# Two remainder tiles of the second experts put into one stationary tile, more last blocks kept on chip, and the mask built later

## The chip, the cores and the metric

One core of one Trainium2 chip runs the kernel. The metric is the device time of the kernel in microseconds (us); lower is better. Three runs of the kernel before gave 1200.51, 1204.14 and 1206.46 us, so the median is 1204.14 us.

## What is computed

Two graph layers on 625 nodes of 256 features with 20,000 edges. Each layer is an attention over edges, a mixing part and a mixture-of-experts part that sends each node to its two best experts. This change touches the two expert parts and the mask that lies between them.

```python
# first experts: 16 experts, hidden size 512; second experts: 8 experts, hidden size int(8/3*256) = 682
hidden = silu(h1) * h2                       # h1 = x @ w1[e], h2 = x @ w2[e]
expert_out = hidden @ w3[e]                  # weighted by the router's two best and summed
...
e = einsum('ehd,ehd->eh', q[src], k[dst]) * scale       # second layer's attention, over edges only
ex = exp(e - segment_max(e, dst)[dst])
...
hh = silu(flat @ w1[e].T) * (flat @ w3[e].T)            # second experts
out = out + weights[:, e:e + 1] * (hh @ w2[e].T)
```

## The kernel before, in words

**Experts as blocks.** The function `experts` exists once for each engine and is called for "e0" (first experts) and "e1" (second experts). The 1250 choices (625 nodes, two each) are laid out in blocks of 128 slots, each block of one expert: 25 blocks in e0 (`NBLK0`), 17 in e1 (`NBLK1`). `block_steps` runs blocks 0 to 3 unrolled, then loops over four at a time, and then the last ones unrolled (from block 20 in e0, from block 12 in e1). So every engine has a `step(b)`, and the engines meet through semaphores alone.

**One step of TensorE.** `row_nodes(b+3)` makes the node numbers of a later block, `turn_rows(b+1)` transposes the gathered rows of the next block (L737), `hidden(b)` makes the two input products (L750), and `output(b-1)` makes the output product of the block before (L761). All products are float32; the trace shows two records for each. In e1 the hidden size 682 gives five tiles of 128 columns and one of 42 (`TILES1`), in two units: tiles 0 to 3, then tiles 4 and 5 (`UNITS1`). `hidden` goes through the unit for q=0 (into banks 1 and 2) and then for q=1 (banks 3 and 4). So in each block's second unit TensorE does: tile 4 and tile 5 of the first matrix, tile 4 and tile 5 of the second, each for two halves k of the 256 inputs.

**One step of VectorE.** In this order: `node_ids(b+3)` (L1528, cast of the node numbers, from which GpSimd gathers that block's rows), `select(b+4)`, the product of silu and the second matrix (L1541), `copy_y(b-1)` (L1572, the output of the block before, out of PSUM), and for the last blocks `spread_rows(b)` (two operations at L1561 and one at L1565, which make a 128x625 matrix of weights that brings the block's slots back to the nodes). The first `spread_rows` waits for `row_info`.

**ScalarE and the row information.** ScalarE copies the turned rows (L1879), makes silu (L1899), and stores the output of a finished block to DRAM (L1884, `slot_y`). `fetch_info` (L1917) loads `row_info`, two rows of 1250 numbers broadcast to 128 partitions, at the start of ScalarE's step 20 in e0 and step 12 in e1.

**The two ways back to the nodes.** Outputs of the early blocks are stored to `slot_y`; when the last of these stores has landed, GpSimd issues ten indirect gathers from it (L2085, in `choices`, after the row gathers of all blocks on the same queue), and VectorE adds them to x in five pairs (L1595). Outputs of the last `KEPT` blocks (4 in e0, 2 in e1) stay on chip: TensorE multiplies each by its weight matrix (`combine`, L783, five products for a block) into PSUM, and VectorE adds these sums (L1599) after the gathered ones. Then come the layer normalization (e0) or the output (e1).

**The weights.** SyncE loads each block's input weights (`exw`, L2190) into one of two slots as soon as `hidden` of the block two before is done, and its output weights (L2181). One float32 row of e1's input weights has 4 x 682 = 2728 numbers.

**The mask.** `cnt` holds the logarithm of edge counts. After its last block in e0, and before `copy_y(24)`, VectorE makes a bfloat16 mask in `mask_words` (five operations, L1586) and turns `cnt` into the additive mask of the second layer's attention (five more, L1589).

**What follows e0.** Layer normalization, `to_fm("xnT2")` on TensorE, `from_fm("xnT2")` on ScalarE and VectorE (L959), then products "gq" and "gk" (L486), whose second halves VectorE takes out of PSUM (L1614, L1618).

Of the kernel before, what the change touches and what calls it, by code (L numbers as in the profile page):

```python
# [20 lines left out]
ALU = mybir.AluOpType  # L21
# [9 lines left out]
N, D, E = 625, 256, 20000  # L31
# [73 lines left out]
FOLDS = 5  # L105
KEPT = {"e0": 4, "e1": 2}
PLAIN = 4
NBLK0 = (2 * N - NE0) // SLOTS + NE0
HT0, HT1 = 128, 128
TILES0 = [(m, min(HT0, HID0 - m * HT0)) for m in range((HID0 + HT0 - 1) // HT0)]  # L110
TILES1 = [(m, min(HT1, HID1 - m * HT1)) for m in range((HID1 + HT1 - 1) // HT1)]
UNITS0 = [TILES0]
UNITS1 = [TILES1[:4], TILES1[4:]]
# [56 lines left out]
def build(nc, x_in, src_in, dst_in, rows_in, vec0_in, vec1_in, fb_in, w0_in, w1_in, w2_in, mixw_in, exp0_in,  # L170
          exp0o_in, exp1_in, exp1o_in, exp1r_in, rope_in, out):
    ctx = ExitStack()
    with ctx:
# [149 lines left out]

        exw = arena[:, 0:2 * 4 * HID1].rearrange("p (s n) -> p s n", s=2)
        at = 2 * 4 * HID1
        exo = arena[:, at:at + 2 * 5 * D].rearrange("p (s n) -> p s n", s=2)
# [30 lines left out]
        def y_of(k, s):  # L357

            return ys[:, s, :] if k < 2 else ys_last[:, k - 2, :]

# [81 lines left out]
        def _(pe):  # L442
# [271 lines left out]

            def experts(name, nblk, units, w_in, w_out, n_out):

# [24 lines left out]
                def hidden(b, s):  # L741
                    pe.wait_ge(sem(f"{name}_in{s}"), (b - s) * 8 + 16)
                    pe.wait_ge(sem(name + "_xsT"), b + 1)
                    for j, tiles in enumerate(units):
                        buf = j if nu == 2 else s
                        after(pe, sem(name + "_mul"), b * nu + (j - 1))
                        for q in range(2):
                            for i, (m, rows) in enumerate(tiles):
                                for k in range(K2):
                                    mm = pe.matmul(banks[1 + 2 * q + buf][0:rows, i * SLOTS:(i + 1) * SLOTS],  # L750
                                                   w_in(s, q, k, m, rows), xsT[:, s, k, :],
                                                   start=(k == 0), stop=(k == 1))
                        mm.then_inc(sem(name + "_hid"), 1)
# [21 lines left out]
                def combine(b, s):  # L775
# [6 lines left out]
                    for t in range(T):  # L782
                        pe.matmul(kept_sum(t), row_hots[:, k, t * P:(t + 1) * P], y_of(k, s), start=(k == 0),  # L783
                                  stop=True, skip_group_check=True).then_inc(sem("combined"), 1)
# [95 lines left out]
            def l2_scores(i, m, h):  # L880

                for c, off, w, _ in chunks_upto(m + 1):
# [15 lines left out]
            experts("e1", NBLK1, UNITS1,  # L898
                    lambda s, q, k, m, rows: exw[:, s, (q * 2 + k) * HID1 + m * HT1:(q * 2 + k) * HID1 + m * HT1 + rows],
                    lambda s, m: exo_r[:, s, :] if m == 5 else exo[0:HT1, s, m * D:(m + 1) * D], 2)  # L900


        @block.vector
        def _(dve):
# [581 lines left out]
            def experts(name, nblk, units, shift_logits, shares, then):  # L1486
# [43 lines left out]
                def step(b, q):  # L1530
# [6 lines left out]
                    for j, tiles in enumerate(units):  # L1537
                        buf = j if nu == 2 else s
                        dve.wait_ge(sem(name + "_silu"), b * nu + (j + 1))
                        for i0, m0, n, rows in runs(tiles):  # L1540
                            ins = v.tensor_tensor(hid[0:rows, s, m0:m0 + n, :],  # L1541
                                                  banks[3 + buf][0:rows, i0 * SLOTS:(i0 + n) * SLOTS]
                                                  .rearrange("p (m n) -> p m n", n=SLOTS),
                                                  silu[0:rows, buf, i0:i0 + n, :], ALU.mult)
# [8 lines left out]
                def spread_rows(b):  # L1553
# [4 lines left out]
                    after(dve, sem("spread"), kept_before(name) + k)  # L1558
                    first, second = (f.rearrange("p (t n) -> p n t", t=T) for f in (row_hots[:, k, :], other_hots))
                    for j, hots in enumerate((first, second)):  # L1560
                        own.note(v.scalar_tensor_tensor(hots, rows_slot[j], slot_cols[:, k:k + 1], rows_weight[j],  # L1561
                                                        ALU.is_equal, ALU.mult))
                    own.fence()
                    first = row_hots[:, k, :]
                    v.tensor_tensor(first, first, other_hots, ALU.add).then_inc(sem("spread"), 1)  # L1565
# [17 lines left out]
                block_steps(dve, nblk, step)  # L1583
                if name == "e0":
                    for m in range(T):
                        own.note(v.tensor_scalar(nmask[:, m, :], cnt[:, m, :], -1.0, -BIG, ALU.is_lt, ALU.mult))  # L1586
                    own.fence()
                    for m in range(T):
                        own.note(v.scalar_tensor_tensor(cnt[:, m, :], cnt[:, m, :], HD ** 0.5, nmask[:, m, :], ALU.mult,  # L1589
                                                        ALU.add))  # L1590
                copy_y(nblk - 1, (nblk - 1) % 2)
# [17 lines left out]
            layernorm(x, xn, 1e-5, (sem("xn"), 3 * T), stats_of=())  # L1609
            from_fm("xnT2", fa)  # L1610
            for c, (off, w, _) in enumerate(CHUNKS):
                bank, freed = got(dve, ("gq", 1, c))
# [128 lines left out]
        def _(act):  # L1741
# [129 lines left out]
            def experts(name, nblk, units):  # L1871
# [15 lines left out]
                def step(b, q):  # L1887
# [6 lines left out]
                    for j, tiles in enumerate(units):  # L1894
                        buf = j if nu == 2 else s
                        act.wait_ge(sem(name + "_hid"), b * nu + (j + 1))
                        after(act, sem(name + "_mul"), b * nu + (j - 1))
                        for i0, m0, n, rows in runs(tiles):
                            ins = a.activation(silu[0:rows, buf, i0:i0 + n, :],  # L1899
                                               banks[1 + buf][0:rows, i0 * SLOTS:(i0 + n) * SLOTS]  # L1900
                                               .rearrange("p (m n) -> p m n", n=SLOTS), ACT.Silu)
# [395 lines left out]
```

## Time and profile before

| | |
|---|---|
| median of three runs | 1204.14 us (1200.51 to 1206.46) |
| the profiled execution's own time | 1199.38 us |
| its span in the trace | 1197.6 us |
| TensorE busy | 958.0 us, 80% |
| VectorE busy | 857.0 us, 72% |
| ScalarE busy | 465.5 us, 39% |
| GpSimd busy | 466.9 us, 39% |
| input weights of e1, each block | 1364 KB, 17 loads |
| input weights of e0, each block | 1024 KB, 25 loads |

Times in the trace count from the start of the span. A row of the timeline has the start, the duration, the engine, the line, the operation, what is written and read, the count of merged records, and in brackets how long the engine was idle before and what ended it. Consecutive matmuls overlap, so the distance from start to start tells what one costs, and not the duration. The first experts run from about 644 to 803 us, the second from about 1022 to 1183 us.

### The profile page before, as it was taken

Reading aid. Unit: us, or ns where it says so; the run is one execution under the profiler, and the core shown is the slowest. Engines: PE = TensorE matmul, PEld = TensorE weight load, DVE = VectorE, ACT = ScalarE, POOL = GpSimd, SP = SyncE. Lnnn points to the kernel's source line nnn. Section 1 sums busy time; section 2 is a strip of 40 time slices with the busy share of each in tenths; the row PEclk is TensorE's granted clock in tenths of the full one; section 3 lists DMA queues with packets and bytes.
Section 4 is the critical chain, followed back from the end, with each engine's and each line's share of the span. In section 5 each row is a group of like instructions: output and inputs, shape, how many; then the busy total and the mean of one; then the engine's idle time right before and its main releaser. Section 6 shows DMA issues by size and latency. Waiting matters only on the chain. (4 is left out here: it accounts for less than half of the span.)

```text
span 1197.6 us, 19285 instructions
## 1 busy us (share of the span) xinstructions
PE 958.0 (80%) x6570; PEld 829.1 (69%) x6570; DVE 857.0 (72%) x1934; ACT 465.5 (39%) x791; POOL 466.9 (39%) x374
## 2 busy tenths in 40 slices
PE   4277999679989889974736999976891894999995
PEld 2256798568878778854735999864691683788884
DVE  5457459869887779887987888584879547655514
ACT  1154565557859577527511111101460260111110
POOL 2437878887787778850002222150000000211104
PEclk9688999889999999997866999997996896899998
DMA  8942232322322222129505999870000002777763
GB/s 284 292 145 69 52 73 55 83 47 60 74 62 58 61 61 69 34 44 245 142 22 192 335 322 323 319 246 22 1 2 0 1 2 71 260 268 264 268 240 93
DMA packets 58236, 157.47 MB, mean 131 GB/s; under 512 B 23830, under 2 KB 33227, under 8 KB 49907
## 3 DMA queue, kind: packets, MB, share of 16 engines
q1 hardware_dynamic: 25500, 116.04, 29.8%
q0 software_dynamic: 25056, 24.10, 9.0%
q10 hardware_dynamic: 7610, 16.46, 4.1%
q8 instruction: 37, 0.61, 0.2%
q14 instruction: 33, 0.26, 0.1%
HBM read 136.12 MB, written 20.12 MB: 130 GB/s over the span
## 5 line engine op out<-in xcount | busy, mean ns | idle before, releaser
L2075 POOL DMA_INDIRECT arena<-row_tab,ids x42 | 57.8, 1376 | 503.2 <-DVE ids L1528 500.6
L2030 POOL DMA_INDIRECT pair_scores<-sc_ring,idx_ring x160 | 213.6, 1335 | 61.9 <-issue 48.0
L750 PE MATMUL bank<-arena 128*128 128x128 f32 (+1 forms) x1616 | 200.6, 282 | 3.2 <-DMA arena<-in_exp 3.2
L750 PEld LDWEIGHTS bank<-arena 128*128 128x128 f32 (+1 forms) x1616 | 188.0, 190 | 12.2 <-DMA arena<-in_exp 4.4
L2020 POOL DMA_INDIRECT arena<-xl_tab,idx_ring x120 | 157.9, 1316 | 91.8 <-issue 37.5
L1763 ACT ACTIVATE arena<-fmaps,node_neg 125x875 f32<-125x875 int32 x100 | 100.2, 1023 | 33.8 <-PE bank L524 14.5
L761 PE MATMUL bank<-arena 128*128 128x256 f32 (+1 forms) x404 | 99.2, 388 | 0.5 <-DMA arena<-in_exp0o 0.5
L1767 ACT ACTIVATE late_ohT<-arena 125x875 fp32r<-125x875 f32 x100 | 90.7, 927 | 0.0
L1899 ACT ACTIVATE arena<-bank 128x512 f32<-128x512 f32 (+2 forms) x76 | 32.4, 450 | 140.9 <-PE bank L750 140.9
L524 PE MATMUL bank<-late_hi,late_ohT 125*125 125x256 f32 x500 | 84.3, 298 | 1.4 <-DVE arena L1000 0.8
L761 PEld LDWEIGHTS bank<-arena 128*128 128x128 f32 (+1 forms) x404 | 72.0, 190 | 17.3 <-issue 9.0
L1541 DVE TENSOR_TENSOR arena<-bank,arena 128x512 f32<-128x512 f32 (+2 forms) x76 | 37.2, 509 | 57.5 <-ACT arena L1899 57.5
L502 PE MATMUL bank<-tab 125*128 125x314 bf16 x400 | 62.4, 307 | 19.2 <-DVE tab L1036 18.1
L524 PE MATMUL bank<-late_lo,late_ohT 125*125 125x256 f32 x500 | 76.3, 282 | 0.0
L502 PE MATMUL bank<-tde 125*128 125x314 bf16 x400 | 62.1, 306 | 16.3 <-DVE tde L1036 15.6
L524 PEld LDWEIGHTS bank<-late_hi,late_ohT 125*125 125x125 f32 x500 | 68.8, 191 | 4.6 <-issue 2.3
L1835 ACT ACTIVATE arena<-arena,rneg 125x625 f32<-125x625 f32 (+4 forms) x60 | 44.9, 748 | 57.4 <-DVE rneg L1326 23.7
L524 PEld LDWEIGHTS bank<-late_lo,late_ohT 125*125 125x125 f32 x500 | 66.7, 187 | 0.2
L677 PE MATMUL bank<-ident,arena 125*125 125x125 f32 x260 | 43.6, 301 | 26.5 <-ACT arena L1835 25.8
L1879 ACT ACTIVATE arena<-bank 128x256 f32<-128x256 f32 x42 | 16.1, 384 | 119.5 <-DVE arena L1572 87.1
L524 PE MATMUL bank<-late_hi,early_ohT 125*125 125x256 f32 x300 | 51.5, 305 | 13.9 <-issue 7.7
L502 PEld LDWEIGHTS bank<-tab 125*128 125x128 bf16 x400 | 37.4, 101 | 35.8 <-DVE tab L1036 16.8
(330 smaller groups left out, 1977.0 us busy)
## 6 DMA issues: line engine op xcount, KB each, us to landing
arena<-in_exp SPq DMA_DIRECT2D x25, 1024.0 KB
arena<-in_exp SPq DMA_DIRECT2D x17, 1364.0 KB
arena<-in_exp0o SPq DMA_DIRECT2D x25, 512.0 KB
arena<-in_exp1o SPq DMA_DIRECT2D x17, 640.0 KB
fmaps<-in_rows SPq DMA_DIRECT2D x20, 437.5 KB
arena<-pair_scores SPq DMA_DIRECT2D x7, 1093.8 KB
pair_scores<-cnt SPq DMA_DIRECT2D x5, 1093.8 KB
pair_scores<-cnt ACTq DMA_DIRECT2D x5, 1093.8 KB
```

The source lines that it names most:

```text
L502: mm = pe.matmul(banks[m][:, 0:CW], oh_dst[s][:, j, m * P:m * P + 128], oh_src[s][:, j, :], start=start and j == 0, stop=True, skip_group_ ...
L524: mm = pe.matmul(banks[T + r][0:P, i * D:(i + 1) * D], hot[late, s][:, t, at * P:(at + 1) * P], part[:, t, :], start=(n == 0 and t == 0), ...
L677: mm = pe.transpose(bank[0:P, t * P - off:t * P - off + P], prob[:, i % 3, t * P:(t + 1) * P], ident[0:P, 0:P])
L750: mm = pe.matmul(banks[1 + 2 * q + buf][0:rows, i * SLOTS:(i + 1) * SLOTS], w_in(s, q, k, m, rows), xsT[:, s, k, :], start=(k == 0), stop= ...
L761: mm = pe.matmul(banks[5 + s][:, 0:D], hid[0:rows, s, m, :], w_out(s, m), start=(m == 0), stop=(m == len(flat) - 1))
L1541: ins = v.tensor_tensor(hid[0:rows, s, m0:m0 + n, :], banks[3 + buf][0:rows, i0 * SLOTS:(i0 + n) * SLOTS] .rearrange("p (m n) -> p m n", n ...
L1763: a.activation(apart[late, s][:, t, :], edge_row[late, s][0:P, :], ACT.Abs, bias=node_neg[:, t:t + 1]).then_inc(sem("apart"), 1)
L1767: ins = a.activation(hot[late, s][:, t - 1, :], apart[late, s][:, t - 1, :], ACT.Relu, scale=-1.0, bias=1.0)
L1835: a.activation(prob[:, i % 3, 0:w], masked[:, i % 3, 0:w], ACT.Exp, bias=rneg[:, i:i + 1], scale=-1.0, accum_out=rden[:, i:i + 1]).then_in ...
L2020: p.indirect_dma_start(out=gat[:, b % 2, 0, j * D:(j + 1) * D], out_offset=None, in_=xl_tab, in_offset=bass.IndirectOffsetOnAxis(ap=idx_ri ...
L2030: p.indirect_dma_start(out=pair_scores[which], in_=sc_ring[:, b % 2, j, :], in_offset=None, out_offset=bass.IndirectOffsetOnAxis(ap=idx_ri ...
L2075: p.indirect_dma_start(out=xs[:, q, :], out_offset=None, in_=tab, in_offset=bass.IndirectOffsetOnAxis(ap=ids[:, q, :], axis=0))\
```

## The change

It has three parts.

1. **Packed remainder.** The 42 last columns of both input matrices of e1 are laid beside each other: columns 0 to 41 hold those of the second matrix (`wgate`), 42 to 63 are zeros, 64 to 105 hold those of the first (`win`). `hidden` makes one product of 106 columns for each k into the first matrix's bank when q is 0, and skips the tile when q is 1. ScalarE reads partitions 64 to 105 of that bank for silu and VectorE partitions 0 to 41 for the product. A row of weights has 4 x 640 + 2 x 106 = 2772 numbers, so each load is 1386 KB, and the buffers behind it in the arena move.
2. **Kept blocks.** `KEPT` is 5 in e0 and 3 in e1. The fifth block's weight matrix and output lie in `mask_words`. So blocks 20 to 24 and 14 to 16 are kept, and one block less is stored.
3. **Mask later.** Since `mask_words` is in use till the end of e0, the ten mask operations move behind `from_fm("xnT2")` on VectorE.

```diff
-KEPT = {"e0": 4, "e1": 2}
+KEPT = {"e0": 5, "e1": 3}
...
+REST1, REST_AT = HID1 % HT1, 64
+PACKED = REST_AT + REST1
+IN0, MAIN1 = 4 * HID0, HID1 - REST1
+IN1 = 4 * MAIN1 + 2 * PACKED
...
-            return ys[:, s, :] if k < 2 else ys_last[:, k - 2, :]
+            return ys[:, s, :] if k < 2 else ys_last[:, k - 2, :] if k < 4 else mask_words[:, N:N + D]
+        def hots_of(k):
+            return row_hots[:, k, :] if k < 4 else mask_words[:, 0:N]
...
                         for q in range(2):
                             for i, (m, rows) in enumerate(tiles):
+                                if rows < 128:
+                                    for k in range(K2 if q == 0 else 0):
+                                        pe.matmul(banks[1 + buf][0:PACKED, i * SLOTS:(i + 1) * SLOTS],
+                                                  w_rest(s, k), xsT[:, s, k, :], start=(k == 0), stop=(k == 1))
+                                    continue
...
-                                                  banks[3 + buf][0:rows, i0 * SLOTS:(i0 + n) * SLOTS]
+                                                  banks[(3 if rows == 128 else 1) + buf][0:rows, i0 * SLOTS:(i0 + n) * SLOTS]
...
+                            at = 0 if rows == 128 else REST_AT
-                                               banks[1 + buf][0:rows, i0 * SLOTS:(i0 + n) * SLOTS]
+                                               banks[1 + buf][at:at + rows, i0 * SLOTS:(i0 + n) * SLOTS]
...
                 block_steps(dve, nblk, step)
-                if name == "e0":
-                    for m in range(T):
-                        own.note(v.tensor_scalar(nmask[:, m, :], cnt[:, m, :], -1.0, -BIG, ALU.is_lt, ALU.mult))
-                    own.fence()
-                    for m in range(T):
-                        own.note(v.scalar_tensor_tensor(cnt[:, m, :], cnt[:, m, :], HD ** 0.5, nmask[:, m, :], ALU.mult,
-                                                        ALU.add))
                 copy_y(nblk - 1, (nblk - 1) % 2)
...
             from_fm("xnT2", fa)
+            for m in range(T):
+                own.note(v.tensor_scalar(nmask[:, m, :], cnt[:, m, :], -1.0, -BIG, ALU.is_lt, ALU.mult))
+            own.fence()
+            for m in range(T):
+                own.note(v.scalar_tensor_tensor(cnt[:, m, :], cnt[:, m, :], HD ** 0.5, nmask[:, m, :], ALU.mult,
+                                                ALU.add))
...
-        w_in = np.concatenate([w.reshape(n_exp, K2, 128, hidden).transpose(0, 2, 1, 3).reshape(n_exp, 128, -1)
-                               for w in (win, wgate)], axis=2)
+        by_half = lambda w: w.reshape(n_exp, K2, 128, -1).transpose(0, 2, 1, 3).reshape(n_exp, 128, -1)
+        parts = [by_half(w[:, :, :main]) for w in (win, wgate)]
+        if main < hidden:
+            apart = np.zeros((n_exp, D, REST_AT - (hidden - main)), win.dtype)
+            parts.append(by_half(np.concatenate([wgate[:, :, main:], apart, win[:, :, main:]], axis=2)))
+        w_in = np.concatenate(parts, axis=2)
```

## Rows read from the trace of the kernel before

**Rows 1.** The page, part 1: busy time and share of each engine

```profile
PE 958.0 (80%) x6570; PEld 829.1 (69%) x6570; DVE 857.0 (72%) x1934; ACT 465.5 (39%) x791; POOL 466.9 (39%) x374
```

**Rows 2.** Busy time by stretch; last three: granted clock, DMA share, GB/s

```profile
640.00:740.00 100.00, 97.44 (x744) 91.93 (x742) 82.83 (x180) 18.24 (x36) 25.60 (x19) 0.95 0.92 313
...
1040.00:1140.00 100.00, 100.00 (x689) 83.59 (x689) 56.48 (x132) 15.16 (x43) 15.32 (x11) 1.00 0.74 264
```

**Rows 3.** Timeline of TensorE in e1, input products of two consecutive blocks

```profile
1121.20 5.95 PE L750 MATMUL bank<-arena 128*128 128x128 f32 x48
...
1130.36 5.95 PE L750 MATMUL bank<-arena 128*128 128x128 f32 x48
```

**Rows 4.** L750 alone in one e1 block, cut at starts of records: PE, PEld

```profile
1057.13:1061.04 3.91, 3.91 (x36) 3.91 (x36) 1.00 0.97 398
1061.04:1061.81 0.77, 0.77 (x8) 0.46 (x6) 1.00 1.07 322
1061.81:1062.25 0.44, 0.44 (x5) 0.44 (x4) 1.00 0.06 19
1062.25:1063.01 0.76, 0.76 (x7) 0.45 (x5) 1.00 0.00 0
```

**Rows 5.** Timeline of TensorE, records of L761 behind that block's input products

```profile
1063.01 0.70 PE L761 MATMUL bank<-arena 128*128 128x256 f32 x2
```

**Rows 6.** Timeline of TensorE at the end of e0

```profile
772.11 5.46 PE L750 MATMUL bank<-arena 128*128 128x128 f32 x32 [2.45 <-DMA arena<-in_exp]
...
790.58 1.99 PE L761 MATMUL bank<-arena 128*128 128x256 f32 x8 [0.46 <-DMA arena<-in_exp0o]
792.41 6.64 PE L783 MATMUL bank<-arena,fmaps 128*125 128x256 f32 x30
```

**Rows 7.** Timeline of TensorE at the end of e1

```profile
1178.59 4.58 PE L783 MATMUL bank<-arena,fmaps 128*125 128x256 f32 x20
```

**Rows 8.** The chain that ended last, its step from a store to landing

```profile
1158.07 5.88 DMA slot_y<-arena
```

**Rows 9.** Timeline of GpSimd at the end of e1, first and last gather of ten

```profile
1171.38 1.23 POOL L2085 DMA_INDIRECT arena<-slot_y,sloti  x1 [29.81 <-DMA slot_y<-arena]
...
1186.18 1.22 POOL L2085 DMA_INDIRECT arena<-slot_y,sloti  x1 [0.31 <-issue]
```

**Rows 10.** Timeline of VectorE at the end of e1

```profile
1179.66 2.04 DVE L1595 SCALAR_TENSOR_TENSOR x<-arena,wstored,x 125x256 f32<-125x256 f32 x4
...
1190.47 1.00 DVE L1595 SCALAR_TENSOR_TENSOR x<-arena,wstored,x 125x256 f32<-125x256 f32 x2 [2.03 <-DMA arena<-slot_y,sloti]
1191.51 2.24 DVE L1599 TENSOR_TENSOR x<-x,bank 125x256 f32<-125x256 f32 x5
```

**Rows 11.** Timeline of VectorE at the end of e0 and behind it

```profile
763.58 0.15 DVE L1528 CAST ids<-bank 128x1 int32<-128x1 f32 x1
...
773.89 1.36 DVE L1561 SCALAR_TENSOR_TENSOR fmaps<-fmaps,slot_cols 128x625 f32<-128x625 f32 x1 [3.99 <-DMA fmaps<-slot_rows]
...
776.47 0.81 DVE L1565 TENSOR_TENSOR fmaps<-fmaps,arena 128x625 f32<-128x625 f32 x1
...
793.79 2.28 DVE L1586 TENSOR_SCALAR mask_words<-cnt 125x625 bf16<-125x625 f32 x5
796.11 3.69 DVE L1589 SCALAR_TENSOR_TENSOR cnt<-cnt,mask_words 125x625 f32<-125x625 f32 x5
...
804.19 3.09 DVE L1595 SCALAR_TENSOR_TENSOR x<-arena,wstored,x 125x256 f32<-125x256 f32 x6 [2.10 <-DMA arena<-slot_y,sloti]
...
825.48 2.23 DVE L1614 TENSOR_SCALAR arena<-bank,fbias 64x375 f32<-64x375 f32 x4 [5.49 <-PE bank L486]
```

**Rows 12.** Timeline of GpSimd at the end of e0

```profile
764.53 0.95 POOL L2075 DMA_INDIRECT arena<-row_tab,ids  x1 [4.10 <-DVE ids L1528]
778.39 1.23 POOL L2085 DMA_INDIRECT arena<-slot_y,sloti  x1 [12.91 <-DMA slot_y<-arena]
...
795.32 1.45 POOL L2085 DMA_INDIRECT arena<-slot_y,sloti  x1 [0.31 <-issue]
```

**Rows 13.** DMA issues from 740 to 815 us: count, size, issue to landing

```profile
vec<-in_vec SPq DMA_DIRECT2D x1, 1665.0 KB, 18.0
```

More of the change, by code:

```diff
@@ L111 @@
 TILES1 = [(m, min(HT1, HID1 - m * HT1)) for m in range((HID1 + HT1 - 1) // HT1)]
+REST1, REST_AT = HID1 % HT1, 64
+PACKED = REST_AT + REST1
+IN0, MAIN1 = 4 * HID0, HID1 - REST1
+IN1 = 4 * MAIN1 + 2 * PACKED
+assert 0 < REST1 <= REST_AT
 UNITS0 = [TILES0]
@@ L322, in build @@
         assert at + 2 * K2 * N <= 4 * H * N
-        exw = arena[:, 0:2 * 4 * HID1].rearrange("p (s n) -> p s n", s=2)
-        at = 2 * 4 * HID1
+        exw = arena[:, 0:2 * IN1].rearrange("p (s n) -> p s n", s=2)
+        at = 2 * IN1
         exo = arena[:, at:at + 2 * 5 * D].rearrange("p (s n) -> p s n", s=2)
@@ L713, in _, with experts @@
             attend("l0", None, lambda t, h: xlr[:, t, h * HD:h * HD + VW], all_tiles)
-            def experts(name, nblk, units, w_in, w_out, n_out):
+            def experts(name, nblk, units, w_in, w_out, n_out, w_rest=None):
                 nu = len(units)
@@ L782, in combine @@
                     for t in range(T):
-                        pe.matmul(kept_sum(t), row_hots[:, k, t * P:(t + 1) * P], y_of(k, s), start=(k == 0),
+                        pe.matmul(kept_sum(t), hots_of(k)[:, t * P:(t + 1) * P], y_of(k, s), start=(k == 0),
                                   stop=True, skip_group_check=True).then_inc(sem("combined"), 1)
@@ L898, in _ @@
             experts("e1", NBLK1, UNITS1,
-                    lambda s, q, k, m, rows: exw[:, s, (q * 2 + k) * HID1 + m * HT1:(q * 2 + k) * HID1 + m * HT1 + rows],
-                    lambda s, m: exo_r[:, s, :] if m == 5 else exo[0:HT1, s, m * D:(m + 1) * D], 2)
+                    lambda s, q, k, m, rows: exw[:, s, (q * 2 + k) * MAIN1 + m * HT1:(q * 2 + k) * MAIN1 + m * HT1 + rows],
+                    lambda s, m: exo_r[:, s, :] if m == 5 else exo[0:HT1, s, m * D:(m + 1) * D], 2,
+                    lambda s, k: exw[:, s, 4 * MAIN1 + k * PACKED:4 * MAIN1 + (k + 1) * PACKED])
         @block.vector
@@ L1558, in spread_rows @@
                     after(dve, sem("spread"), kept_before(name) + k)
-                    first, second = (f.rearrange("p (t n) -> p n t", t=T) for f in (row_hots[:, k, :], other_hots))
+                    first, second = (f.rearrange("p (t n) -> p n t", t=T) for f in (hots_of(k), other_hots))
                     for j, hots in enumerate((first, second)):
@@ L1563, in spread_rows @@
                     own.fence()
-                    first = row_hots[:, k, :]
+                    first = hots_of(k)
                     v.tensor_tensor(first, first, other_hots, ALU.add).then_inc(sem("spread"), 1)
```

## The prediction

> **What bounds the kernel now.** I read the page first: TensorE is the busiest engine, at 80% [rows 1]. The share is an average, so I then read the busy times by stretch. In the second experts (e1) TensorE is busy for all of 100 us at the full clock, and DMA has room, a share of 0.74 at 264 GB/s. In the first experts (e0) TensorE is busy 97.44 of 100 us and DMA is nearly full, 0.92 at 313 GB/s [rows 2]. So e1 is set by TensorE, and e0 by TensorE with DMA just behind. Then come the two ends. The chain that ended last shows how e1 ends: a store, gathers from it, five pairs of additions, five sums. The last pair waits 2.03 us for its gather [rows 10]. At the end of e0 the additions also wait for gathers [rows 11].
>
> **Part 1, the packed remainder.** The blocks of e1 follow each other every 9.16 us (1130.36 - 1121.20) [rows 3], with no idle time between, so what leaves a block leaves the time, 17 times. I cut one block's 48 records of L750 at starts of records [rows 4]. The first 35 starts, all of 128 columns, take 3.91 us: 0.112 each. The next window holds the start of one wide record and of the four narrow ones (42 columns): 0.77 us where five at 0.112 would be 0.56, so +0.21. The third holds three wide starts and takes 0.44 where 0.335 would do, +0.10: the first wide record behind the narrow group is late as well. The fourth repeats the second, +0.20 to +0.21. The output product behind it repeats the third: its first two records take 0.70 us [rows 5], of which a record's duration of 0.38 is the end, so they start 0.32 apart, and not 0.216 (30 records of the same kind in 6.64 us, less one duration, give 29 distances of 0.216 [rows 6]): +0.10. From this, a narrow group costs 4 x 0.112 = 0.447 for its records and 0.31 for going from wide to narrow and back.
>
> Per block the change removes one group whole: 0.447 + 0.31 = 0.76 us. The other becomes 106 columns wide. Whether it keeps its 0.31 has no row. From below the nearest is 42 columns, which pays it; from above 125 columns, which doesn't: L783 (125) starts at 792.41, and the last L761 (128) started at 790.58 + 1.99 - 0.38 = 792.19, so 0.22 apart, the usual distance [rows 6]. I take the upper row, because 106 is nearer to 125 than to 42. Then a block saves 0.76 + 0.31 = 1.07 us, and 17 blocks 18.2 us; with the 0.31 kept it is 17 x 0.76 = 12.9 us.
>
> The Trainium skill, TensorEngine Tiling (Array Packing), Key Properties and Performance Considerations, says that a change of tiling mode drains the engine and puts column tiling at a stationary side of 64 columns or fewer. By that rule the 42-column groups drain and the 106-column group does not; the trace agrees as far as it goes (42 pays 0.31, 125 nothing), and the sum by the rule is the same 18.2 us.
>
> What could take the place of TensorE in a block of 8.08 us? Its loads grow by 22 KB on 1364. DMA moves 264 x 9.16 = 2.42 MB in a block; with 0.02 more in 8.08 us this is 302 GB/s, a share of 0.74 x 9.16 / 8.08 x 1.01 = 0.85, below what e0 sustains [rows 2]. VectorE is busy 56.48 of 100 us, 5.2 us a block. Reading from partition 64 has no row; I take it at nothing, as the reads are as large as before, and hold them off the path, since the output product of a block starts a whole input product later. If each cost 0.2 us more they would still be covered.
>
> **Part 2 in e1.** Three kept blocks mean that the last store is that of block 13, and not 14. It is issued at 1158.07 and takes 5.88 us to land [rows 8]. By then 15 of 17 packed blocks lie behind it, so it comes at 1158.07 - 15 x 1.07 = 1142.0 and lands at 1147.9; GpSimd starts 0.28 us later, 1148.2. Its ten issues take 1187.40 - 1171.38 = 16.0 us [rows 9], till 1164.2; the last pair of additions began 3.07 us behind the last issue [rows 9, 10], so it begins at 1167.3. TensorE and VectorE come from the other side: x is ready for additions at 1179.66 - 18.2 = 1161.5, and four pairs at 1.02 us are through by 1165.5, so the last gather still decides. Last pair at 1167.3 against 1190.47: 23.2 us, that is 18.2 of part 1 and 5.0 of this one. The additional `spread_rows(14)` (3.4 us, as 773.89 to 777.28 [rows 11]) lies in VectorE's idle time. The additional five products, 10 x 0.216 = 2.2 us, start at 1178.59 - 18.2 = 1160.4 [rows 7], so three blocks' are through at 1167.1, before the sums begin at 1168.3. Were store 13 to take a third less or more, 4 to 7.8 us, this term would be 6.8 (there VectorE, and not the gather, is last) to 3.1.
>
> **Part 2 in e0: a wait moved in front of a gather.** The store of block 20 goes, so the gathers could start sooner than 778.39 [rows 12]. But block 20 now needs its weight matrix, so VectorE waits for `row_info` in step 20, and the fetch is issued where it was. It landed at 773.89 [rows 11]. Before, that wait stood in step 21, behind `node_ids(24)`. Now it stands ahead of it. Queued behind the waiting instruction are the three operations (till 777.3), then `node_ids(24)`, done at 763.58 before, and the product of block 21. For `node_ids(24)` wait the row gather of block 24, which GpSimd issues 0.95 us later [rows 11, 12], and behind that on the same queue the ten gathers back: 777.3 + 0.95 + 0.95 to 1.41 + 0.3 gives 779.5 to 779.9. They start 1.1 to 1.5 us later than before, not earlier. TensorE waits for block 24's rows in front of `hidden(23)`: gather issued by 779.4, landed some 3 us later, so about 3.7 us late. Its products for kept blocks start at 792.41 + 3.7 = 796.1 and take 5 x 2.16 = 10.8 us, till 806.9. The big loads behind the last weights (the one of 1665 KB lands 18.0 us after issue [rows 13]) move back with it and hold the last gathers as before. So additions end about 1.5 us later than the 807.3 of before, at 808.8, and TensorE's 806.9 stays covered; with 1.7 us more for a low clock after the wait (5.46 us for the 32 records at 772.11 behind such a wait [rows 6], against 32 x 0.112 + 0.16 = 3.74) it is just covered. I take +1.5, within 0 and +4. A gain isn't excluded: the early gathers leave DMA before the big loads start, so down to -2.
>
> **Part 3, the mask.** Its 2.28 + 3.69 us stood in front of `copy_y(24)`, but `spread_rows(20)` has eaten that room and the additions wait for gathers anyway: 0 there. In its new place VectorE is idle for 5.49 us before 825.48 [rows 11]; 5.97 us in it makes L1614 0.5 us late, and that is made up before the next product needs a bank. Without that cover it would cost 6 us. I take 0, up to 0.5.
>
> **The sum.** -18.2 - 5.0 + 1.5 + 0 = -21.7 us. Against the profiled execution (1199.38, span 1197.6) it gives 1177.7, span 1175.9. The median of the runs is 4.8 us above the profiled one, so I forecast 1204.14 - 21.7 = 1182.4 us.
>
> **The rivals.**
> 1. *The packed tile still pays for the change of width.* For it: no row at 106 columns. Against: 125 pays nothing. A block saves 0.76, store 13 is issued at 1158.07 - 15 x 0.76 = 1146.7, and by the steps above the last pair begins at 1171.9, 18.5 us ahead of 1190.47. -18.5 + 1.5 = -17.0: 1187.1 us. Chance 0.12.
> 2. *The end of e0 gains as part 2 wants it.* It happens if the row information lands some 5 us sooner: then the first gather starts at about 775 instead of 778.39, and the end of e0 gains about 3 us: -23.2 - 3 = -26.2, 1178 us. For it: the landing hangs on how DMA is loaded just then. Against: the change takes no traffic from before 773.89. Chance 0.08.
> 3. *Packing gains nothing*, since something other than TensorE sets e1's blocks, and 100% busy hides it. Only the ends move, -5.0 + 1.5: 1200.6 us. Against: no idle time between blocks, and full clock. Chance 0.04.
> 4. *Slower: the loads.* The second weight slot begins 11,088 bytes into the arena row and not 10,912, in e0 as well, where DMA is at 0.92. Should these transfers slow down, e0's 25 blocks lengthen at once. It decides from 21.7 / 25 = 0.87 us a block. A block of e0 moves 1024 + 512 + 128 + 128 KB = 1.84 MB, 5.9 us at 313 GB/s; 0.87 more is 272 GB/s. At 235 GB/s it is 7.8 us, 25 x 1.9 = 48 us more, 1230 us. Against: nothing in the trace sets the slots apart. Chance 0.02.
>
> **How the numbers follow.** My forecast, 1182.4, has 0.74. A measurement of this kernel tells 0.5% (6 us) from no change. Cases 1, 2 and the forecast are faster by more: 0.94; case 3 is the same, 0.04; case 4 slower, 0.02. The range goes from case 2 less the runs' own 3 us (1175) to case 1 with e0 at +4 and a little of the same (1191).
>
> **What would show it.** In the changed profile e1's blocks should come every 8.1 us with 44 records of L750 in 4.9 us (8.4 us with rival 1, 9.2 with rival 3). The first gather of e1's end should start about 1148, and the last pair of additions wait for a gather. At the end of e0 the cast of block 24's ids should sit behind L1565 at 777, the first gather back near 780, with TensorE idle ahead of L737. The mask should fill VectorE's idle stretch behind L959, and L486's records should be as close as before. The prediction fails if e1's blocks are bound by loads at over 8.5 us, or if row information lands at another time.

## The result and the profile after

The changed kernel takes 1181.42 us (median of four runs, 1179.06 to 1185.43), the kernel before on the same chip 1203.12 us (four runs). The ratio is 0.9837, 95% interval 0.9809 to 0.9865: 19.6 us faster, between 16 and 23. A second set of rounds gave 0.9827 (0.9797 to 0.9857). The forecast was 1182.4 us and 21.7 us faster, in the range of 1175 to 1191. The profiled execution is one of the longer ones of its kernel: 1183.17 us, span 1181.4, against 1199.38 and 1197.6 before.

**The blocks of e1.** The timeline of TensorE, as [rows 3] has it for the kernel before. L764 is now the line of the wide input products, L760 that of the packed one, L775 that of the output product:

```profile
1122.65 4.18 PE L764 MATMUL bank<-arena 128*128 128x128 f32 x36
1126.67 0.60 PE L760 MATMUL bank<-arena 128*106 128x128 f32 x4
1127.11 0.61 PE L764 MATMUL bank<-arena 128*128 128x128 f32 x4
1127.55 2.95 PE L775 MATMUL bank<-arena 128*128 128x256 f32 x12
...
1130.73 4.18 PE L764 MATMUL bank<-arena 128*128 128x128 f32 x36
```

A block comes every 8.08 us (1130.73 - 1122.65), where it was 9.16. The 44 records take 4.90 us (1127.55 - 1122.65). The group of 106 columns takes 0.44 us (1127.11 - 1126.67), four times 0.11, with nothing on either side: it pays nothing for the change of width. The output product is 0.10 shorter as well. One small remainder stays: the output product's last two records have only 42 rows of weights. From the record ahead to the first of them it is 0.31 us, to the second 0.32, and to what follows 0.31, where the other records start 0.216 apart. That is 0.29 us in each block, in both kernels, and no run took it away.

The same stretch by busy times, beside the second row of [rows 2] (columns: TensorE, its weight loads, VectorE, ScalarE, GpSimd, granted clock, DMA share, GB/s):

```profile
1040.00:1140.00 100.00, 100.00 (x728) 88.84 (x727) 59.43 (x138) 18.80 (x49) 16.29 (x12) 1.00 0.86 311
```

TensorE is still busy all the time, and DMA went from 0.74 to 0.86 without a wait.

**The end of e1.** The chain's step from the store, then GpSimd and VectorE, as [rows 8, 9, 10]. L2100 are the gathers, L1603 the additions, L1607 the sums:

```profile
1147.13 5.70 DMA slot_y<-arena
```

```profile
1154.08 1.23 POOL L2100 DMA_INDIRECT arena<-slot_y,sloti  x1 [21.29 <-issue]
1155.62 1.79 POOL L2100 DMA_INDIRECT arena<-slot_y,sloti  x1 [0.30 <-issue]
1157.71 1.85 POOL L2100 DMA_INDIRECT arena<-slot_y,sloti  x1 [0.30 <-issue]
...
1164.42 2.04 POOL L2100 DMA_INDIRECT arena<-slot_y,sloti  x1 [0.30 <-issue]
...
1170.02 1.21 POOL L2100 DMA_INDIRECT arena<-slot_y,sloti  x1 [0.30 <-issue]
```

```profile
1166.60 3.08 DVE L1603 SCALAR_TENSOR_TENSOR x<-arena,wstored,x 125x256 f32<-125x256 f32 x6
...
1174.26 1.01 DVE L1603 SCALAR_TENSOR_TENSOR x<-arena,wstored,x 125x256 f32<-125x256 f32 x2 [2.00 <-DMA arena<-slot_y,sloti]
1175.30 2.24 DVE L1607 TENSOR_TENSOR x<-x,bank 125x256 f32<-125x256 f32 x5
```

This is the store of block 13, as it was in [rows 8]. Before, though, the gathers waited for the one after it, that of block 14, which was issued at 1167.21 and landed at 1171.10, 0.28 us ahead of the first gather. Now block 13's is the last. The last pair of additions still waits for the last gather. But from the store to that pair it is 27.1 us (1174.26 - 1147.13), where the prediction had 25.3. The store landed at 1152.83 and the first gather began 1.25 us later instead of 0.28, and three of the ten issues take 1.8 to 2.0 us.

**The end of e0.** VectorE, then TensorE, then GpSimd, as [rows 6, 11, 12]. L1576 and L1580 spread rows, L1543 casts block 24's row numbers, L1620 and L1623 are the mask:

```profile
772.79 1.37 DVE L1576 SCALAR_TENSOR_TENSOR fmaps<-fmaps,slot_cols 128x625 f32<-128x625 f32 x1 [7.47 <-DMA fmaps<-slot_rows]
...
776.10 0.15 DVE L1543 CAST ids<-bank 128x1 int32<-128x1 f32 x1
...
808.70 1.01 DVE L1603 SCALAR_TENSOR_TENSOR x<-arena,wstored,x 125x256 f32<-125x256 f32 x2 [3.65 <-DMA arena<-slot_y,sloti]
...
822.34 2.05 DVE L1620 TENSOR_SCALAR mask_words<-cnt 125x625 bf16<-125x625 f32 x5
824.43 3.69 DVE L1623 SCALAR_TENSOR_TENSOR cnt<-cnt,mask_words 125x625 f32<-125x625 f32 x5
828.28 2.23 DVE L1628 TENSOR_SCALAR arena<-bank,fbias 64x375 f32<-64x375 f32 x4 [0.16 <-PE bank L495]
```

```profile
783.10 0.69 PE L746 MATMUL bank<-ident,arena 128*128 128x128 f32 x2 [4.19 <-DMA arena<-row_tab,ids]
783.58 6.30 PE L764 MATMUL bank<-arena 128*128 128x128 f32 x32
...
799.66 8.80 PE L797 MATMUL bank<-arena,fmaps 128*125 128x256 f32 x40
808.30 2.32 PE L797 MATMUL bank<-mask_words 128*125 128x256 f32 x10
```

```profile
777.06 0.95 POOL L2090 DMA_INDIRECT arena<-row_tab,ids  x1 [15.26 <-DVE ids L1543]
778.31 1.22 POOL L2100 DMA_INDIRECT arena<-slot_y,sloti  x1 [0.30 <-issue]
```

SyncE's queue, the issue of the first big load behind e0's weights (2184 KB), before and after:

```profile
785.38 0.43 SPq L2207 DMA_DIRECT2D wres<-in_w  x1
792.16 0.43 SPq L2222 DMA_DIRECT2D wres<-in_w  x1
```

The wait for the row information has moved ahead of the cast, as the prediction said. The cast comes at 776.10 and not at 763.58, the row gather of block 24 behind it, and on the same queue, 0.30 us behind, the first gather back. TensorE stands 4.19 us before it can turn block 24's rows, and the 32 records after it take 6.30 us. The sums begin 2.4 us later than before in the two profiles. The mask's ten operations fit into the idle stretch with 0.16 us left.

The two spans differ by 16.2 us and not by 21.7. From the second block's transposition in e1 to the last block's the change gains 14.5, from there to the last sum 5.3. It loses 2.4 up to the last sum of e0 and 1.2 between there and the second block of e1.

### The profile page after: what moved, and what is told of

The parts are those of the page before. It is cut to its first block and busy times, and to the rows that moved or that the text cites. A ratio compares the mean times of both kernels' runs of the same rounds, so it can differ in the third digit from the quotient of the medians.

```text
span 1181.4 us, 19195 instructions
## 1 busy us (share of the span) xinstructions
PE 952.1 (81%) x6522; PEld 835.4 (71%) x6522; DVE 861.0 (73%) x1940; ACT 468.0 (40%) x791; POOL 467.8 (40%) x374
## 5 line engine op out<-in xcount | busy, mean ns | idle before, releaser
L764 PE MATMUL bank<-arena 128*128 128x128 f32 x1480 | 183.5, 283 | 3.2 <-DMA arena<-in_exp 3.1
L764 PEld LDWEIGHTS bank<-arena 128*128 128x128 f32 x1480 | 177.8, 199 | 5.6 <-DMA arena<-in_exp 4.4
L775 PE MATMUL bank<-arena 128*128 128x256 f32 (+1 forms) x404 | 97.7, 384 | 1.3 <-DMA arena<-in_exp0o 0.9
L775 PEld LDWEIGHTS bank<-arena 128*128 128x128 f32 (+1 forms) x404 | 72.1, 190 | 15.2 <-issue 6.6
L686 PEld LDWEIGHTS bank<-ident,arena 125*125 125x125 f32 x260 | 40.0, 215 | 29.6 <-issue 18.3
```

Source lines behind the costliest of these rows:

```text
L686: mm = pe.transpose(bank[0:P, t * P - off:t * P - off + P], prob[:, i % 3, t * P:(t + 1) * P], ident[0:P, 0:P])
L775: mm = pe.matmul(banks[5 + s][:, 0:D], hid[0:rows, s, m, :], w_out(s, m), start=(m == 0), stop=(m == len(flat) - 1))
```

## The experiments

Every kernel ran in five rounds beside the kernel before, but the three of width have one execution each. Ratios are to the kernel before on the same chip, in brackets with the 95% interval.

### The parts alone

**Packing alone**: the changed kernel with the old numbers of kept blocks, and the ten mask operations back ahead of `copy_y(nblk - 1)`.

```diff
-KEPT = {"e0": 5, "e1": 3}
+KEPT = {"e0": 4, "e1": 2}
...
+                if name == "e0":
+                    for m in range(T):
...
                 copy_y(nblk - 1, (nblk - 1) % 2)
```

> Part 1 alone: the packed remainder, with KEPT 4 and 2 and the mask in its old place. Theory (TensorE sets the blocks of e1, and a group of 42 columns pays for the change of width): blocks of e1 every 8.07 us instead of 9.15, 17 blocks, 17 to 18 us faster than the kernel before. If the gain of the changed kernel came as much from the blocks kept on chip, this one is only 14 to 16 us faster. If the lower gain at the start of e1 (seen in one profile) is of the change itself, the first two blocks save nothing here too.

Ratio 0.9845 (0.9818 to 0.9872), 18.6 us faster on 1197.5, between 15.3 and 21.8. Blocks of e1 come every 8.07 us, as in the changed kernel. Part 1 alone is nearly the whole gain. The forecast's term was 18.2.

**One more kept block in e1 alone**: the kernel before with one number changed.

```diff
-KEPT = {"e0": 4, "e1": 2}
+KEPT = {"e0": 4, "e1": 3}
```

> One more kept block in e1 alone (KEPT 4 and 3), nothing else. Forecast term: 5.0 us faster. The profile of the changed kernel points to 3.1 us, since the gathers back come earlier but take longer while VectorE spreads rows. Rival (the end of e1 is set by the products of the kept blocks): no gain.

Ratio 0.9952 (0.9931 to 0.9972), 5.7 us faster, between 3.4 and 8.3. The forecast's 5.0 lies in it; the 3.1 that the first profile pointed to lies just outside. VectorE's last additions wait 0.46 us for the gather, where three pairs waited some 2 us each in [rows 10] and before it:

```profile
1179.92 4.12 DVE L1595 SCALAR_TENSOR_TENSOR x<-arena,wstored,x 125x256 f32<-125x256 f32 x8
1184.50 1.01 DVE L1595 SCALAR_TENSOR_TENSOR x<-arena,wstored,x 125x256 f32<-125x256 f32 x2 [0.46 <-DMA arena<-slot_y,sloti]
```

From the transposition of the last block's rows to the last sum it is 29.6 us in this profile against 35.8 before. In the packed kernels the same stretch is 34.2 us with two kept blocks (one profile) and 29.0 to 30.5 with three (the first four such profiles). So by the profiles the term is 6.2 us without packing and 3.6 to 5.1 with it: the shorter blocks let TensorE and VectorE arrive sooner, and the chain of ten gathers, which packing doesn't shorten, is what is left.

**One more kept block in e0 with the mask later**, without packing; `y_of`, `hots_of` and the place of the mask are as in the change.

```diff
-KEPT = {"e0": 4, "e1": 2}
+KEPT = {"e0": 5, "e1": 2}
...
```

> One more kept block in e0 (KEPT 5 and 2) and with it the mask behind the turned rows, no packing. Theory (the wait for the row information now stands ahead of block 24's row numbers): 1 to 3 us slower than the kernel before, the last pair of additions in e0 1 to 3 us later. Rival (the earlier last store lets the gathers start sooner): 2 to 3 us faster.

Ratio 1.0032 (1.0011 to 1.0052): 3.8 us slower, between 1.3 and 6.2. The waits that the prediction names are there, VectorE's and TensorE's:

```profile
770.94 1.36 DVE L1565 SCALAR_TENSOR_TENSOR fmaps<-fmaps,slot_cols 128x625 f32<-128x625 f32 x1 [7.77 <-DMA fmaps<-slot_rows]
```

```profile
781.96 0.69 PE L741 MATMUL bank<-ident,arena 128*128 128x128 f32 x2 [4.68 <-DMA arena<-row_tab,ids]
```

The one profile doesn't place the whole 3.8 us. A stretch that can be compared is that from the transposition of block 22's rows to the last sum of e0. It is 47.6 us here, 47.4 in the kernel before, 46.3 in the run above and 44.4 in the next.

**The mask later alone**, four and two blocks kept: the ten operations go from ahead of `copy_y(nblk - 1)` to behind `from_fm("xnT2")`.

```diff
                 block_steps(dve, nblk, step)
-                if name == "e0":
-                    for m in range(T):
...
                 copy_y(nblk - 1, (nblk - 1) % 2)
...
             from_fm("xnT2", fa)
+            for m in range(T):
...
```

> The mask moved behind the turned rows alone, KEPT 4 and 2, no packing. Theory (the additions at the end of e0 wait for gathers anyway, and the new place is idle): within 1 us of the kernel before. Rival (the mask held back the last output's copy and the additions): up to 4 us faster. Rival (its new place delays the products taken out of PSUM): up to 2 us slower.

Ratio 0.9982 (0.9957 to 1.0007): nothing that this can tell from no change, though a gain of up to 5.1 us would not be excluded either. The run before this one differs from it by the fifth kept block alone: the medians are 1201.52 and 1197.18, 4.3 us apart. VectorE came to its additions at 790.73, 7 to 9 us sooner than the 797.68 and 800.05 of the two unpacked profiles with the mask in front, and gave 5.65 us of that back waiting:

```profile
793.85 1.00 DVE L1588 SCALAR_TENSOR_TENSOR x<-arena,wstored,x 125x256 f32<-125x256 f32 x2 [1.07 <-DMA arena<-slot_y,sloti]
799.43 2.05 DVE L1588 SCALAR_TENSOR_TENSOR x<-arena,wstored,x 125x256 f32<-125x256 f32 x4 [4.58 <-DMA arena<-slot_y,sloti]
```

In its new place the mask shows no cost: from the last sum of e0 to the first transposition of e1 it is 208.5 to 211.6 us in the ten profiles with the mask there, and 209.3 to 211.4 in the four with it in front.

The parts add up: -18.6 - 5.7 + 3.8 = -20.5 us; the whole change was measured at -19.6 and, in the next set, -20.8. Each part is known to 2.5 or 3.2 us either way, so the sum is no test of a microsecond.

### What the kept block in e0 costs, and what holds the gathers

**The changed kernel again**, beside the next two.

> The changed kernel once more, beside the next two on one chip: 18 to 23 us faster than the kernel before. Shows whether the longer half clock at the start of e1 is of the change or of the run.

Ratio 0.9827 (0.9797 to 0.9857), median 1180.98. On the start of e1: from the second block's transposition to the last block's it takes 121.1 us in four packed profiles (this kernel's first one, packing alone, KEPT 4 and 3, fetch at 16) and 119.7 in this one. Unpacked it is 135.6 in the first profile before and 137.1 in three others. So there are two lengths, some 1.5 us apart, in either kind. They go with the granted clock (1.00 is full, 0.50 half). It stands at 0.50 when the second block's rows are transposed. In the short profiles it is back at 1.00 some 2.9 us later, in the long ones 5.8 to 6.0 us later, and 3 us at half clock make up the 1.5. The profile before is a short one and the first after a long one, which hides 1.5 us of the gain: between long and long it is 137.1 - 121.1 = 16.0 = 15 x 1.07.

**KEPT 4 and 3 with packing**, the mask's ten operations in front, where they were before the change.

```diff
-KEPT = {"e0": 5, "e1": 3}
+KEPT = {"e0": 4, "e1": 3}
...
+                if name == "e0":
+                    for m in range(T):
...
```

> The changed kernel with KEPT 4 in e0 and the mask in its old place; 3 kept in e1 and the packing stay. Theory (the fifth kept block costs at the end of e0): 1 to 3 us faster than the changed kernel. Rival (it is worth what was wanted): 2 to 3 us slower than the changed kernel.

Ratio 0.9818 (0.9789 to 0.9847), 1179.46 us. It is 1.5 us below the changed kernel's median, and the intervals overlap: the direction fits the theory, the measurement doesn't settle it. What speaks for it is the fifth block's cost without packing, and the profiles. From the first transposition in e0 to its last sum it is 166.9 us here, and 166.4 to 170.8 in all five profiles with four kept blocks up to this one, against 170.0 to 173.8 in the six with five and the row information at block 20 (twice the changed kernel, the one without packing, and the three of width below). Part of that spread lies ahead of block 22, before a kept block matters. From block 22's transposition on it is 43.9 to 47.4 us with four and 46.9 to 48.6 with five, on average 2.8 us more.

**The row information fetched at block 16** of e0 instead of 20.

```diff
-    quads = (nblk - 8) // 4
+    quads = (nblk - 8) // 4 - (nblk == NBLK0)
...
-                    if static and b == 4 + (nblk - 8) // 4 * 4:
+                    if static and b == (16 if nblk == NBLK0 else 12):
```

> The changed kernel with the fetch of the row information issued at block 16 of e0 instead of 20 (all engines run blocks 16 to 19 unrolled). Theory (the wait for it in step 20 costs the end of e0): VectorE has no wait ahead of L1576 in step 20, the first gather back starts 2 to 4 us sooner, TensorE doesn't wait 4 us for block 24's rows, and the kernel is 3 to 7 us faster than the changed one. Rival (the gathers are held by the big loads behind the weights whatever their start): within 1 us of the changed kernel.

Ratio 0.9811 (0.9778 to 0.9844), 1177.81 us: 3 us below the changed kernel by median, with intervals that overlap. The theory had 3 to 7 us and its rival up to 1, and the time alone doesn't tell them apart. The mechanism is seen in the trace. VectorE has no wait ahead of its first spread, TensorE waits 0.49 us and not 4.19 for block 24's rows, and the first gather back starts at 773.73 and not at 779.46 (the changed kernel on this chip). The end of e0 is shorter: from block 22's transposition to the last sum it is 42.3 us, and 48.2 and 48.4 in the two profiles of the changed kernel. So in the profiles the end of e0 gains about the 5.7 us of the sooner start, and the stretch ahead of block 22 happened to be long in this one (126.0 us, where the other thirteen have 122.0 to 125.4). But the gathers land late again:

```profile
767.49 1.36 DVE L1576 SCALAR_TENSOR_TENSOR fmaps<-fmaps,slot_cols 128x625 f32<-128x625 f32 x1
...
795.11 3.08 DVE L1603 SCALAR_TENSOR_TENSOR x<-arena,wstored,x 125x256 f32<-125x256 f32 x6
804.03 2.05 DVE L1603 SCALAR_TENSOR_TENSOR x<-arena,wstored,x 125x256 f32<-125x256 f32 x4 [5.84 <-DMA arena<-slot_y,sloti]
```

VectorE now waits 5.84 us for gathers whose issue was over at 791.4. They lie in DMA beside the loads of 2184 and 1665 KB, which were issued at 785.0 and 785.5 and landed at 797.4 and 804.1.

**These loads held** until the last gather has landed, on top of that.

```diff
             sp.wait_ge(sem("e0_routed"), 3)
+            sp.wait_ge(sem("back4"), 2 * 16)
             sp.dma_start(wres[:, :, 0:W_SIZES[1]], w1_in).then_inc(sem("w1_in"), 16)
```

> The kernel with the row information fetched at block 16, and the two big loads behind e0's weights (wres 2184 KB, vec 1665 KB) held until the last gather back has landed. Theory (these loads hold the gathers, which is why sooner gathers gave nothing): no wait of VectorE for gathers, additions end by 801, and the sums, now behind TensorE's products of kept blocks, end about 4 us sooner than without the hold; 4 us faster than the kernel fetched at 16. Rival (the loads are needed sooner than 820): TensorE waits ahead of L495 and the gain is lost.

Ratio 0.9784 (0.9753 to 0.9814), 1175.68 us: 3.2 us less than without the hold by the ratios, with intervals that overlap. All five pairs of additions run without a wait, and then VectorE waits for TensorE's products of the kept blocks:

```profile
793.85 5.16 DVE L1603 SCALAR_TENSOR_TENSOR x<-arena,wstored,x 125x256 f32<-125x256 f32 x10
801.23 0.42 DVE L1607 TENSOR_TENSOR x<-x,bank 125x256 f32<-125x256 f32 x1 [2.22 <-PE bank L797]
```

```profile
800.09 2.32 PE L797 MATMUL bank<-mask_words 128*125 128x256 f32 x10
```

TensorE doesn't wait for the weights ahead of L495. So the loads held the gathers. Once they are out of the way, what VectorE waits for at the end of e0 is TensorE's products, and the ten records that one kept block more puts there take 2.2 us, about this wait. From block 22's transposition to the last sum it is 41.1 us, 1.2 less than without the hold: most of the 5.84 us passed to other waits.

**Four kept blocks, mask later, loads held**: the version that this points to.

```diff
-KEPT = {"e0": 5, "e1": 3}
+KEPT = {"e0": 4, "e1": 3}
...
+            sp.wait_ge(sem("back4"), 2 * 16)
```

> Packing, KEPT 4 in e0 and 3 in e1, mask in its late place, and the two big loads held until the last gather has landed. Theory (mask off the end of e0, four kept blocks there, gathers not held): the sums of e0 end 5 to 8 us sooner than with KEPT 4 and 3 alone; 5 us faster than that kernel, about 1174 us. Rival (the end of e0 hangs on when the row information lands): no more than 2 us.

Ratio 0.9767 (0.9733 to 0.9801), 1173.62 us, the lowest of all kernels that ran: below the changed kernel's two ratios by 0.7 and 0.6%, with intervals that meet at their edges. Beside KEPT 4 and 3 with the mask in front and no hold (0.9818) it is 6.1 us, where 5 was expected; these intervals overlap by a little too. The stretch from block 22's transposition is 37.6 us, against 43.9 in that kernel. The additions wait 0.40 us, the sums follow at once:

```profile
796.87 1.00 DVE L1603 SCALAR_TENSOR_TENSOR x<-arena,wstored,x 125x256 f32<-125x256 f32 x2 [0.40 <-DMA arena<-slot_y,sloti]
797.91 0.42 DVE L1607 TENSOR_TENSOR x<-x,bank 125x256 f32<-125x256 f32 x1
```

By this trace, moving the mask is now worth some 5.6 us: in front of the additions its 6 us would have only the wait of 0.40 us to hide in. That is an estimate. No run had the loads held and the mask in front, so how the 6.1 us divide between the two edits isn't shown.

### The price of the narrow group by itself

Three kernels make the packed product a second time at q=1, into a part of the other bank that nobody reads, with 106, 65 or 64 columns.

```diff
                                 if rows < 128:
-                                    for k in range(K2 if q == 0 else 0):
-                                        pe.matmul(banks[1 + buf][0:PACKED, i * SLOTS:(i + 1) * SLOTS],
-                                                  w_rest(s, k), xsT[:, s, k, :], start=(k == 0), stop=(k == 1))
+                                    wide = PACKED if q == 0 else 65
+                                    for k in range(K2):
+                                        mm = pe.matmul(banks[1 + 2 * q + buf][0:wide, i * SLOTS:(i + 1) * SLOTS],
+                                                  w_rest(s, k)[:, 0:wide], xsT[:, s, k, :], start=(k == 0), stop=(k == 1))
```

> The changed kernel with the packed product made a second time, at q=1, into a bank part that nobody reads: 106 columns. Theory (a change to 64 columns or fewer costs, 106 doesn't): blocks of e1 every 8.07 + 0.45 = 8.52 us. Rival (106 pays for the change too, hidden in the numbers of the changed kernel): 8.8 us.

> The changed kernel with the packed product made a second time at q=1 for its first 65 columns, into a bank part that nobody reads. Theory (the price belongs to 64 columns or fewer): blocks of e1 every 8.51 us, as with 106. Rival (it belongs to narrow tiles in general and fades with width): between 8.6 and 8.8 us.

> The same with its first 64 columns. Theory: the change of width is paid, blocks of e1 every 8.51 + 0.31 = 8.82 us. Rival (only the 42 columns' odd size pays): 8.51 us.

TensorE's timeline, first of the kernel with 65, then of that with 64 (the line numbers differ by one from the changed kernel's):

```profile
1078.67 4.18 PE L765 MATMUL bank<-arena 128*128 128x128 f32 x36
...
1083.12 0.61 PE L765 MATMUL bank<-arena 128*128 128x128 f32 x4
1083.57 0.60 PE L761 MATMUL bank<-arena 128*65 128x128 f32 x4
1084.01 2.95 PE L776 MATMUL bank<-arena 128*128 128x256 f32 x12
...
1087.18 1.50 PE L765 MATMUL bank<-arena 128*128 128x128 f32 x12
```

```profile
1082.06 4.18 PE L765 MATMUL bank<-arena 128*128 128x128 f32 x36
...
1086.51 0.61 PE L765 MATMUL bank<-arena 128*128 128x128 f32 x4
1087.05 0.65 PE L761 MATMUL bank<-arena 128*64 128x128 f32 x4
1087.63 3.05 PE L776 MATMUL bank<-arena 128*128 128x256 f32 x12
...
1090.91 1.28 PE L765 MATMUL bank<-arena 128*128 128x128 f32 x10
```

Blocks come every 8.51 us with 106 and with 65 columns, and every 8.85 us with 64. From the four wide records to the group of 64 it is 0.54 us (1087.05 - 1086.51) where the group of 65 comes after 0.45; from that group to L776 it is 0.58 and not 0.44; and L776 takes 3.05 and not 2.95. One column fewer costs 0.34 us a block. These are distances within a trace, alike in all blocks of e1 at full clock. The whole times, one each, are 1191.47 us with 106 columns, 1190.52 with 65 and 1187.68 with 64, and say nothing of it: the kernel with 64 came to e1 5 to 6 us sooner than the other two. The Trainium skill, TensorEngine Tiling (Array Packing), puts column tiling at 64 columns or fewer and says that a change of mode drains the engine (Performance Considerations; Key Properties). The threshold is as these runs have it. That it is a drain which costs the 0.34 us, no trace shows.

## Why the prediction was right

- **Part 1, 18.2 us: right in mechanism and size.** 44 records in 4.90 us, blocks every 8.08 us, 18.6 us by itself in a run of its own. The value taken for 106 columns, that of 125, held, and the runs with 65 and 64 columns show where the line lies. This rules out rival 1 (8.4 us a block) and rival 3 (9.2).
- **What could take TensorE's place: right.** DMA stands at 0.86 of its time (0.85 was worked out) and nothing waits for it; reading from partition 64 shows no cost on the path. Rival 4, slower loads in e0, would have made 48 us and is out. A small cost of that kind is not: from the first transposition of e0 to that of block 22 it is 122.0 to 124.6 us in the four unpacked profiles and 123.0 to 126.0 in the ten packed ones, 1.6 us more on average.
- **Part 2 in e1, 5.0 us: the mechanism right, the size at its edge.** 5.7 us in a run without packing, 3.6 to 5.1 in the packed profiles. In the first profile two steps were too short: 0.28 us from landing to the first issue (1.25 measured), and 16.0 us for ten issues (17.2, 1154.08 to 1171.23). Together they are 2.1 us.
- **Part 2 in e0, +1.5 us: the mechanism right, the size probably too small.** The order of things came as told: cast behind the spread, row gather, gathers back, TensorE idle. Yet the time of the first gather was wrong by over a microsecond (779.5 to 779.9 foretold, 778.31 measured), because the row information landed sooner, at 772.79. The cost was 3.8 us (1.3 to 6.2) in a run of its own, and 2.4 in the profile. The term that was too small is TensorE's. It resumed at 783.10, 4.0 us late where 3.7 was worked out, and took 6.30 us for the next 32 records, at a granted clock of 0.56. The 1.7 us that the prediction set aside for this became 2.6. So the products of the kept blocks began 7.3 us late and not 3.7. What VectorE waited for in the end were the gathers: the big loads moved back with TensorE, from 785.4 to 792.2, and the last gather landed at 808.6.
- **Part 3, 0: right as far as it can be told**, since the run of its own leaves room from 5.1 us faster to 0.8 slower. The mask fills the idle stretch; in front, it was mostly hidden by the gathers. What it is worth without that cover is an estimate, 5.6 us.
- **Rival 2** (the end of e0 gains if the row information lands sooner) was made to happen by fetching it at block 16. The gathers did start 5.7 us sooner than in the changed kernel, the end of e0 was shorter by some 6 us in the profile, and the time was 1177.81 us, where the rival had 1178. By time alone that can't be told from the changed kernel. The rival didn't name the second hold, the loads behind the weights, which the next run showed.
- The sum was right because its two misses, e0 (2.3 us too little cost) and e1's end with packing (up to 1.4 us too much gain), were small against part 1. They go the same way, and the gain was indeed 1 to 2 us less than forecast. That 1182.4 us came within 1 us of 1181.42 is partly luck: the kernel before, too, was 1 us below the value that the forecast started from.

## What to carry to other kernels

Look at the distances between starts around a group of another width, and not at durations: in this float32 kernel a tile of 64 columns or fewer between wide ones cost a third of a microsecond beyond its own work, and padding it past 64, or packing two remainders into one, took that away. Before keeping one more block on chip, see what its first operation waits for and what stands behind it on that queue. And when a gather that nobody hurries ends a stage, look for a large load issued just before it, and try holding that load.

## What the runs showed of the hardware that was not expected

- **Gathers beside bulk loads.** Counted from the start of its issue, an indirect gather of 125 rows landed after 3.8 to 5.0 us at the end of e1, where no loads are left, and after 9.0 to 17.6 us at the end of e0 while 3.8 MB of loads were in flight (803.07 - 789.34 = 13.7 in the kernel before). With the loads held, the last two of e0 landed after 3.9 and 4.0 us (four kept blocks, mask later).
- **GpSimd issues beside VectorE.** Over all fourteen profiles, of 280 gathers back, 115 were issued with no VectorE operation of over 0.8 us beside them: median 1.21 us, none over 1.5. Of the 165 with such an operation beside them 75 took over 1.6 us. All of these operations read or write 625-element float32 rows in on-chip memory. That the two share something is a guess from this count; no run took the operations away.
- **The first gather of e1's end** came 0.28 to 0.29 us behind the last store's landing in the four profiles with two kept blocks, where an even block is stored last, and 0.90 to 1.25 us behind it in the ten with three. It isn't settled; the order of the two waits in `choices` was not tried.
- **The clock at the start of e1** returned to full at one of two times, 2.8 to 2.9 us (four profiles) or 5.8 to 6.0 us (ten) behind the second block's transposition, in kernels with and without the change. The later one costs 1.5 us.
